# A graph network's edge passes: GpSimd gathers all 28 source columns of a chunk, and TensorE's picks are gone

## The reference

```python
x = _layernorm(x + layer0(x))     # segment_sum of sigmoid(att) * x[dst], then tanh(. @ W)
x = _layernorm(x + layer1(x))     # five graph attention passes (four of one kind, one of [x, h])
x = _layernorm(x + layer2(x))     # one pass of dot-product attention
x = _layernorm(x + layer3(x, e))  # three passes of 4-head attention with edge features
# a pass of layer 1:
h = x @ W;  al = h @ a_src;  ar = h @ a_dst
logit = leaky_relu(al[src] + ar[dst], 0.2)
alpha = segment_softmax(logit, dst)
out = segment_sum(alpha[:, None] * h[src], dst) + b        # then gelu
```

## Time and profile before

| | us |
|---|---|
| median of three timed runs | 10527.93 (10525.65 to 10530.43) |
| span of the profiled execution | 14084.2 |
| GpSimd busy in it | 7724.8 |
| VectorE busy | 7042.7 |
| TensorE busy (matmuls) | 6814.7 |
| ScalarE busy | 5152.3 |

### The profile page before, as it was taken

The page is one execution under the profiler, slowest core; times in us unless marked ns, Lnnn a source line. Parts: engine busy times, 40 slices in busy tenths (PEclk is TensorE's granted clock), DMA queues, the critical chain, the costliest instruction groups (busy, mean ns, idle before and its releaser), DMA issues. The chain is left out here.

```text
span 14084.2 us, 100376 instructions
## 1 busy us (share of the span) xinstructions
PE 6814.7 (48%) x27637; PEld 5669.8 (40%) x27637; DVE 7042.7 (50%) x12322; ACT 5152.3 (37%) x5609; POOL 7724.8 (55%) x7576
## 2 busy tenths in 40 slices
PE   5443366657756774777577646661111322232222
PEld 5433355545545553655455535551111211121111
DVE  5333345434444443444444546663444466646666
ACT  0011144444434443444344424442222243423432
POOL 7888755544444445344444455546665555545553
PEclk7555577768777776887677767775555565556555
DMA  5333322212211221122133323333332344434442
GB/s 154 36 36 33 58 51 58 56 39 55 54 49 42 56 55 42 48 55 55 40 90 91 86 72 97 97 89 89 115 109 96 116 143 136 140 94 141 138 140 81
DMA packets 782270, 1137.56 MB, mean 81 GB/s; under 512 B 500471, under 2 KB 559955, under 8 KB 774499
## 3 DMA queue, kind: packets, MB, share of 16 engines
q0 software_dynamic: 355008, 370.44, 14.1%
q1 hardware_dynamic: 363245, 417.03, 9.6%
q10 hardware_dynamic: 63926, 349.09, 6.2%
HBM read 680.14 MB, written 468.70 MB: 82 GB/s over the span
## 5 line engine op out<-in xcount | busy, mean ns | idle before, releaser
L970 POOL DMA_INDIRECT turned<-d_t,idx x5788 | 5465.9, 944 | 5006.3 <-DVE wide L1426 3228.1
L1115 PE MATMUL banks<-pair,hot 128*128 128x462 f32 x16184 | 3981.1, 402 | 1677.0 <-issue 1661.2
L1115 PEld LDWEIGHTS banks<-pair,hot 128*128 128x128 f32 x16184 | 3357.4, 208 | 2299.7 <-issue 1921.1
L1236 DVE TENSOR_TENSOR wide<-banks,member 128x462 f32<-128x462 f32 x1156 | 689.9, 634 | 2788.3 <-remote 2123.6
L1084 ACT COPY wide<-wide 128x952 f32<-128x952 f32 (+2 forms) x252 | 503.4, 1997 | 2831.5 <-DVE wide L1446 2800.7
L650 POOL DMA_INDIRECT d_acc<-work,idx x784 | 1237.7, 1579 | 263.9 <-issue 234.4
L733 ACT ACTIVATE hot<-keys,row 128x1024 fp32r<-128x1024 f32 (+1 forms) x1036 | 1073.1, 1117 | 277.9 <-PE banks L1115 204.9
L1171 PE MATMUL banks<-ident,wide 128*128 128x128 f32 x588 | 163.1, 423 | 1814.2 <-issue 945.2
L1446 DVE TENSOR_TENSOR_SCAN wide<-banks,wide 128x224 f32<-128x224 f32 (+4 forms) x1288 | 1036.9, 871 | 5.8
L1128 PE MATMUL banks<-pair,hot 128*128 128x448 f32 x3136 | 804.7, 417 | 452.1 <-issue 393.8
L1128 PEld LDWEIGHTS banks<-pair,hot 128*128 128x128 f32 x3136 | 688.1, 221 | 568.7 <-issue 492.5
(11 more groups left out here) (311 smaller groups left out, 9556.1 us busy)
## 6 DMA issues: line engine op xcount, KB each, us to landing
d_e<-wide ACTq DMA_DIRECT2D x168, 924.0 KB
turned<-d_t,idx POOLq DMA_INDIRECT x5788
d_e<-wide ACTq DMA_DIRECT2D x84, 1008.0 KB
wide<-d_b SPq DMA_DIRECT2D x60, 1344.0 KB
keys<-d_key SPq DMA_DIRECT2D x124, 512.0 KB
d_b<-wide SPq DMA_DIRECT2D x28, 1344.0 KB
wide<-d_edge SPq DMA_DIRECT2D x84, 448.0 KB
d_em<-wide ACTq DMA_DIRECT2D x84, 448.0 KB
```

The costliest lines, as they stand in the source:

```text
L970: gp.indirect_dma_start(rows[:, b, k, :], None, table[:, :], offset(idx[:, b, k:k + 1])).then_inc(s["gathered"][b], 16)
L1115: mm = nc.tensor.matmul(ps_cols[i], hot[:, place, i, j, :], flat(g.pair[:, part, j]), start=(j, part) == (0, 0), stop=(j, part) == (SETS - ...
L1236: nc.vector.tensor_tensor(found[:, i - i0], ps_cols[i].rearrange("p (w c) -> p w c", c=SET), mid(member[:, i], TW), ALU.mult).then_inc(pic ...
```

## The change

GpSimd gathers all 28 columns of every chunk in every pass. Everything that served TensorE's picks is removed: the one-hot blocks on ScalarE, the key loads of SP and their table in HBM with its preparation in `prepare`, the masks and reductions on VectorE, the split of the node tables, the ring of the dot pass, and 19320 matmuls. The last two chunks are no longer written out after the loop. What is left of an edge pass is what the multi passes already did.

```diff
@@ gpsimd, edges
-        def gather(t, b, columns):
+        def gather(t, b):
 
             gp.wait_ge(s["rows_used"][b], t + 1)
             gp.wait_ge(s["idx_ready"][b], t + 1)
...
-            for k in range(columns):
+            for k in range(K):
                 gp.indirect_dma_start(rows[:, b, k, :], None, table[:, :],
                                       offset(idx[:, b, k:k + 1])).then_inc(s["gathered"][b], 16)
 
-        if X:
-            gather(0, 0, KG - X * AH)
-            gather(0, 1, KG)
-        with gp.Fori(1 if X else 0, LOOPS) as t:
-            for b in range(2):
-                gather(t, b, KG)
+        pairs(gp, gather)
@@ scalar, edges
-            if X and not dot and more:
-                one_hots(nc, g, act, pk, chunk + AH + 3, (b + AH + 1) % 2)
             act.wait_ge(s["logits_done"], chunk + 1)
...
-            if X and not dot and more:
-                one_hots_end(nc, act, pk, chunk + AH + 3, (b + AH + 1) % 2)
@@ tensor, edges
-                for j in range(SETS):
-                    for part in range(2):
-                        mm = nc.tensor.matmul(ps_cols[i], hot[:, place, i, j, :], flat(g.pair[:, part, j]),
-                                              start=(j, part) == (0, 0), stop=(j, part) == (SETS - 1, 1))
@@ vector, edges
-            v.wait_ge(s["gathered"][b], 16 * (KG * (t + 1) - (X * AH if X and b == 0 else 0)))
+            v.wait_ge(s["gathered"][b], 16 * K * (t + 1))
...
-            if X and not dot and (more or b == 0):
-                take(chunk + AH + 2, 1 - b, KG, 0, EARLY, link)
             v.wait_ge(s["exps_done"], chunk + 1)
...
-            elif X and (more or b == 0):
-                take(chunk + AH + 2, 1 - b, KG, EARLY, X, link)
@@ nodes
-            if pk is not None and gat and j >= late:
-                split(j - late)
```

More of the change, by code:

```diff
@@ L852, in edges @@
     mx, sm, fac = (tiles[n] for n in "mx sm fac".split())
-    if X:
-        picks, keys, hot, member = pk.s, pk.keys[:], pk.hot, pk.member
-        if not dot:
-            found = tiles["found"]
-        HB = 2 if dot else 1
-        AH, AT = pk.ahead, pk.first
-        if dot:
-            ps_cols = [banks[:, 2 * (i % 2):2 * (i % 2) + 2, 0:SET * HALF] for i in range(X)]
-        else:
-            bank_of = [i if i < RING else i - RING // 2 - 1 for i in range(X)]
-            ps_cols = [banks[:, i, 0:SET * TW] for i in bank_of]
     ps_eT, ps_em, ps_both, ps_same, ps_w, ps_keep = (
@@ L908, in _ @@
                 sp.dma_start(gs[:], a["e_norm"].partition_broadcast(P)).then_inc(s["loaded"], 16)
-        for n in range(2, 2 if not X else 3 if dot else AH + 4):
-            sp.wait_ge(picks["hot_made"], HB * (n - 1))
-            sp.dma_start(keys, step_keys(g, X, n + AT)).then_inc(picks["keys_loaded"], 16)
         if clear is not None:
@@ L1020, in _ @@
         act.dma_start(prime[0:1, 0:1], g.d_x[0:1, 0:1]).then_inc(s["stored"], 16)
-        for n in range(2, AH + 3 if X and not dot else 2):
-            one_hots(nc, g, act, pk, n, n % 2, n == 2)
-            one_hots_end(nc, act, pk, n, n % 2)
         for b in range(2):
@@ L1245, in _ @@
             v.sem_inc(s["rows_used"][b], 1)
[L1246 to L1252 removed]
+        v.wait_ge(ready["spread_done"], 16 * C)
+        v.wait_ge(ready["seeded"], 16)
         if clear is not None:
@@ L1320, in spread_em @@
             last.then_inc(s["em_spread"], 1)
-        if X and not dot:
-            link = Link(v, s["first_link"])
-            for n in range(1, AH + 1):
-                at = KG - X * (AH + 1 - n)
-                take(n, 0, at, 0, EARLY, link)
-                take(n, 0, at, EARLY, X, link)
-            take(AH + 1, 0, KG, 0, EARLY, link)
-            v.wait_ge(ready["spread_done"], 16 * C)
-            v.wait_ge(ready["seeded"], 16)
         if wide_rows:
@@ L1337, in _, with one @@
             spread_em(0, 0)
-        if X and not dot:
-            take(AH + 1, 0, KG, EARLY, X, link)
-        def one(t, b, more):
+        def one(t, b):
             chunk = 2 * t + b
@@ L1401, in one @@
                                                         ALU.mult, ALU.max))
-                if dot and (more or b == 0):
-                    wide_take(chunk + 2, 1 - b, 0, link)
             if multi:
@@ L1429, in one @@
                                     ALU.mult).then_inc(s["rows_used"][b], 1)
-            if dot and (more or b == 0):
-                wide_take(chunk + 2, 1 - b, 1, link)
             if update:
@@ L1745, in _ @@
                 finish(j + 1)
-            if pk is not None and gat and j >= late:
-                split(j - late)
-        if pk is not None:
-            for j in range(0 if summing else NG - late, NG):
-                split(j)
     def turned_rows(step, j):
@@ L1897, in layer @@
         ph.now = ph.block()
-        pk = Picks(nc, g, ph, edge["kind"], edge["ahead"], edge.get("cols")) if edge and edge["kind"] in COLS else None
-        ready = nodes(nc, g, ph, banks, turned, wide, pk=pk, **node)
+        ready = nodes(nc, g, ph, banks, turned, wide, **node)
         if edge:
-            edges(nc, g, ph, banks, rows, chunk, ready, pk=pk, **edge)
+            edges(nc, g, ph, banks, rows, chunk, ready, **edge)
 class Graph:
```

296 lines of the change are left out of this document (32 added, 264 removed).

## The result

| | before | after |
|---|---|---|
| median, us | 10528.74 (10525.65 to 10530.43) | 12010.81 (12010.56 to 12013.07) |
| ratio | | 1.1407, 95% interval 1.1390 to 1.1423 |
| span of the profiled execution | 14084.2 | 12009.3 |

The account below looks back on a forecast made before the run. GpSimd's stream of indirect DMAs was taken to bound the kernel nearly end to end. 1581 - 184 - 28 - 26 = +1343 us on 10528 gave 11871, taken as 11860 us; the 8-in-10 range was 11350 to 12000.

Parts of the forecast that it names:

- What bounds the kernel: Whole timed kernel: GpSimd's stream of indirect DMAs bounds it nearly end to end, 9925 of 10528 us.
- The price of a gather: Gat and dot passes: 1268 added gathers at 1.247 us each, +1581 us, all on the path.
- The rival of a cheaper gather: Timed gathers cost less, say a pitch of 1.15 us: 11500 us, or 10570 at 0.944; chance 0.18.
- The rival of picks that bind before and a faster kernel: Gat chunks before take 30 us timed, bound by picks, so the change gains: 10030 us; chance 0.05.
- What comes back: Time the change gives back on GpSimd's path: 184, 28 and 26 us, 238 in all.
- (a): Start of the four later gat passes: GpSimd's 46 us wait each vanishes, -184 us, bounds 0 and 322.
- (b): Dot pass's node part: GpSimd's waits of 6.9 us for each of four groups, copies, split and ring, -28 us.
- (c): Splits in four gat node parts, keys in `start`, dot's first picks: some 4 us in six places, -26 us.
- covered by something I don't see: Rival on the gat passes' starts: they give nothing back, +184 us, so 12050 us; chance 0.05.
- The stalls: Stretches of the trace where recorded engines crawl, about 14 us a gat chunk: taken as the recording's effect, absent from timed runs.
- The signs: Profile after: median 944 ns, 0.30 us behind, waits of some 15 us after 56 gathers, no 80-us start wait, span some 14500.
- The other rule weighed: Gathers beside VectorE: a lighter VectorE would speed them well beyond 42 us; left out, as the rows show no lock.

Follow-up runs that it names:

- e8_fewer_b: Changed kernel with 20 gathers a chunk in gat and 24 in dot, no picks, on a chip without stalls: 10474.32 us, ratio 0.9947.
- e2_clear_only: Kernel before with picks kept in the fifth gat pass alone, all other passes gathering 28 columns, on the chip with stalls: 13707.75 us, ratio 0.9859.
- e6_ahead0_b: Kernel before with picks of the four later gat passes no longer 2 steps ahead, on a chip without stalls: 10559.07 us, ratio 1.0027.
- e10_ahead1: Kernel before with picks of the four later gat passes 1 step ahead instead of 2: 10524.81 us, ratio 0.9993.
- e9_gat_only_b: Kernel before with the dot pass gathering all 28 columns, without picks or ring, on a chip without stalls: 10640.48 us, ratio 1.0104.
- e3_dummy_matmuls: Changed kernel plus 112 matmuls a chunk on constant data in gat passes that nobody waits for, on the chip with stalls: 16347.56 us, ratio 1.1755.
- e12_dummy_b: Changed kernel plus 3136 matmuls in each gat pass that nobody waits for, on a chip without stalls: 12015.78 us against 12013.8 unedited.

## Why the prediction was right, and where it failed

**What bounds the kernel: right.** Without stalls GpSimd's gathers run through each pass, in the kernel before with the waits at four starts and 8 us of short ones in dot, in the kernel after with none; `e8_fewer_b` lies within 2 us of what the stream alone gives.

**The price of a gather: right.** Taken as 1.247 us, measured 1.248, with the 0.30 us behind each. 1268 x 1.248 = 1582 us against the 1581 of the sum. The rival of a cheaper gather is dead, and with it the whole lower part of the range. The rival of picks that bind before and a faster kernel fell with the same row on chips without stalls. On the chip with stalls it lives, which the prediction had not thought possible: `e2_clear_only`, with most of the change, is 1.4% faster there. The prediction's argument that the stall doesn't stretch a gather held for its trace alone: in `e2_clear_only` one takes up to 1.99 us.

**What comes back: mis-sized, and this is the failed step.** 238 us were forecast. Measured are 1582 - 1482 = 100, and the runs place nearly all of them:

| term | forecast | measured |
|---|---|---|
| (a) starts of four gat passes | 184 | 51 (`e6_ahead0_b`), 48 (`e10_ahead1`), 4 x 13.0 in the trace |
| (b), (c) dot pass: ring, first picks | 28 + some 4 | 30 (`e9_gat_only_b`) |
| (c) splits in the four gat node parts | some 17 | 4 x 5 = 20 (trace) |
| (c) the keys in `start` | some 4 | not seen |
| sum | 238 | 101 |

The step that failed is in (a): "Without stalls that next gather is at 3070.5; GpSimd was done with its first 24 at 3024.2 and so waits 46 us." The stalls were taken out between the first pick and the release, and left in ahead of the first pick. The pick's own start, 2981.9, was 48 us late by a stall in the node part, against 11 us for GpSimd (169.5 us from its first collect to the end of the 24 gathers, and 158.2 without stalls). These 37 us taken off leave 9, and the rest of the 12.6 is that from the first pick to the release 91.8 us pass, not 70.2 + 18.3 = 88.5. The 336 matmuls take 72.7 us instead of 70.2, since the first ten run at a granted clock of 0.50 (the row below), and the last column's mask of 0.64 us comes behind them, ahead of the reduction. The row with 34.95 us was in the trace of before and wasn't read. TensorE's first picks in `e9_gat_only_b`, by stretch:

```profile
2608.00:2612.00 4.00, 3.97 (x10) 3.49 (x11) 2.26 (x6) 0.14 (x1) 2.87 (x3) 0.50 0.54 134
2615.20:2681.00 65.80, 65.80 (x315) 59.04 (x315) 25.33 (x32) 38.26 (x27) 49.89 (x53) 1.00 0.17 35
```

184 - 51 = 133 us too much was given back. The other terms were 4 too much together, the gathers 1 too little, and rounding the sum of 11871 down took 11: 11860 + 133 + 4 + 1 + 11 = 12009, 2 us short of the 12011.

The bounds of the term were 0 and 322, and the range didn't carry them: with nothing given back at the starts the prediction named 12050 itself, and closed the range at 12000 with 0.05 for that case. The truth was most of that rival, "covered by something I don't see".

**(b) was right in size and wrong in place.** The waits of 6.9 us a group in the earlier trace rows are not there without stalls: no node scatter of the dot pass waits over 0.3 us for ScalarE's copies (`e6_ahead0_b`). From the join to the first gather the dot pass takes 145.9 us with the ring (`e6_ahead0_b`) and 135.9 after, 10 us, and some 8 of them are what line 767 adds to the seven DMAs beside it. The others are 8 us of waits inside the pass, five of them of 1.6 to 1.8, and 11.5 us at its end, 39.25 against 27.74, which the prediction didn't name.

**The stalls: not of the recording alone.** "3556 us of the trace are not in the timed runs" was right for the runs shown, and the sum could rest on it. "I take these stalls for an effect of the recording" is not borne out as it stands: they are a state of one chip, in all its timed runs, and absent in profiled executions on others. Recording may still have a part in them: every timed run here has a span, so it was recorded too, and no run shows that chip without it. Which condition makes the difference is open. The rule of the Trainium skill, "NOTIFIC — the notification-queue block" (section 7.1, Overflow), that a full pipeline holds its producers back, would fit engines that slow down at independent work, as in `e3_dummy_matmuls`; no run here shows it as the cause.

**The signs.** Seen: the median of 944 ns, 0.30 us behind it, no 80-us wait at a start. Not seen: a wait of 15 us after every 56 gathers and a span of some 14500. The span is 12009.3, since this profile was taken without stalls. The other rule weighed is that of the Trainium skill's "SBUF — State Buffer" (SBUF: two separate sides): a DMA issued from GpSimd can't get its descriptors written while VectorE runs certain copies. It says the same of VectorE instructions with two inputs in SBUF, against a GpSimd instruction that reads SBUF. The prediction took the rule to promise faster gathers from any relief of VectorE. VectorE's busy time fell by 1690 us and the gathers' median stayed at 944 ns. But what ran beside them and left were mostly line 1236's products with the mask and line 1240's reductions, 690 and 602 us, and these have at most one input in SBUF, since `banks` is PSUM: beside them, too, the gathers of `e6_ahead0_b` take 0.94 to 0.96 us. So for the gathers the sum was right to leave the rule out. Such a lock is in this kernel all the same, in the node part: line 767 has both inputs in SBUF, and every DMA that starts beside it ends some 0.7 us after it. The splits' copy, line 766, shows none. The prediction priced the splits at some 4 us a pass without naming this, and the 5 measured hold it.

## What to carry to other kernels

When a trace holds disturbance that the timed runs don't, every time taken from it as a start must be cleaned too, not only the durations after it: follow the chain back to an event that both engines share, here the first collect, and compare from there. What picks on an idle engine are worth is the instructions that they spare the bound one, here 1.248 us a gather; their own cost lies at the edges of the passes, and an experiment that shifts the edge (`ahead` 2, 1, 0) prices it within a few us. And a range should reach the time that one names oneself for a term's own lower bound.

## What the runs showed of the hardware

- One chip runs the kernel before in 13902 us, with a span as long, where three others take 10530 (ratio 1.32). On it TensorE crawls while GpSimd's indirect DMAs run: 18 independent matmuls in 50 us against 258 elsewhere, at an equal count of 41 gathers. The verdict on a change can turn with it: `e2_clear_only` has a ratio of 0.986 there and 1.114 elsewhere.
- On chips without stalls the pitch of an indirect DMA of 128 rows didn't depend on TensorE's load: 1.248 us with it idle (after), 1.249 with it busy with picks (`e9_gat_only_b`), and 1.248 with it busy throughout (`e12_dummy_b`). From one execution to another and from pass to pass it lay between 1.248 and 1.255.
- An indirect DMA of GpSimd that starts while VectorE subtracts one tensor in SBUF from another (line 767) ends 0.68 to 0.75 us after that instruction: 1.21 to 1.44 us instead of 0.94 beside one of 128x462 (25 DMAs of `e9_gat_only_b`), 1.70 to 2.45 beside one of 128x896 (7 of `e6_ahead0_b`). Beside line 1236's product of a tensor in PSUM with one in SBUF it keeps 0.94 to 0.96 (336 of `e6_ahead0_b`), and so it does beside line 1240's reduction of one in SBUF (393).
- TensorE's granted clock is 0.50, its lower level of 1.2 GHz, in a gat pass after, where it has no work, and in the node part behind it; under the dummy matmuls it is 1.00. It costs nothing: the node part's matmuls stood at 0.50 with the picks as well, in the row of 2527 to 2609 above, with 35.61 us of work. The first gat pass after, and the node part behind it, by stretch:

```profile
1764.00:2742.00 978.00, 0.00 (x0) 0.00 (x0) 271.42 (x545) 141.34 (x178) 739.26 (x784) 0.50 0.25 54
2742.00:2896.00 154.00, 35.81 (x151) 29.46 (x151) 41.83 (x134) 38.00 (x56) 97.64 (x103) 0.50 0.13 29
```
